# One core, attention and a gated low-rank block: tile 2 projected from split operands, splits reordered, reciprocals kept in a score bank

## The chip, the cores and the metric

The kernel runs on one core of one Trainium2 chip. The metric is the device time of one execution in microseconds (us). The core has TensorE (matrix products, PE in the profile; PEld is its weight load), VectorE (DVE), ScalarE (ACT), GpSimd (POOL) and SyncE (SP), which issues nearly all transfers here. Each engine works through its own list of instructions in order; semaphores tie the lists together.

## The reference, cut to what matters

1,024 tokens (16 batches of 64) of width 512; `c` is the context, 32 query heads of 16 over 8 key/value heads.

```python
h = layernorm(x)
q, k, v = h @ Wq, c @ Wk, c @ Wv          # 512x512, 512x128, 512x128
q, k = rope(q, pos), rope(k, pos)
x = x + softmax(q k^T / 4) v @ Wo
h = layernorm(x)
gate = softmax over the 16 largest of 64 router scores of h
x = x + 2 * (((h @ A.T) * gate) @ B.T)    # 64 experts of rank 8
```

## The kernel before

**Tiles.** The tokens go in T = 8 tiles of 128. Everything is float32. A product is made in one of two ways. *Raw*: one float32 matmul per 128 rows of the contraction, which the profile shows as two records (`raw_q`, `raw_kv`). *Split*: each operand is written as a high part in `float32r` and the rest (`hi`, `lo`), and three matmuls are made per 128 rows: hi x hi, hi x lo, lo x hi (`project_q`, `project_kv`, `project_out`, `project_down`, `up_high`, `up_low`). ScalarE makes the high parts (`split_hi`, `x_high`, `c_high`), GpSimd the low parts of weights and context (`split_lo`, `c_low`), VectorE those of x (`x_low`). `RAW = 3`: tiles 0 to 2 are raw, tiles 3 to 7 split.

**Order.** Each engine's program is written out by hand: `first()`, `second()`, then `step(i)` for i = 1 to 5, then `last()`. `first()` warms TensorE with 12 bf16 matmuls (`keep_warm`), turns tile 0, and projects tiles 0 and 1. `second()` finishes attention of tile 0 and projects tile 2. In `step(i)` attention of tile i is finished, the scores of i+1 are made, tile i+2 is projected, and the last block runs two tiles behind.

**The o chain of a tile.** `values(t)` (TensorE, L1149) writes the weighted values and the sums into score banks 0 and 1; VectorE transposes them into `o_s` (L789), takes reciprocals `inv` (L794), multiplies into `o_t` (L798, two instructions) and transposes into `o_n` (L804); ScalarE makes `oT_hi` (L507), GpSimd `oT_lo` (L313); TensorE then runs `project_out(t)` (L1053, L1054, L1058). `scores(t, b)` writes banks 2 and 3 for b = 0 and banks 0 and 1 for b = 1. Before b = 1 it waits for

```python
pe.wait_ge(o_step, 3 * t - 2)
```

which is the transposition of tile t-1 out of these banks (each tile gives `o_step` three increments: transposition, reciprocals, multiplication).

**The maxima.** `top(t, b)` (VectorE, L771) takes row maxima of the scores, `m_parts` splits them, `turn_m` (L1122) and ScalarE's `m_out` (L492, `mT`) turn them, and `turned_scores(t)` (L1132, L1138) makes the transposed scores less the maxima, of which `exps` (L499) are taken.

**Banks.** `xhT_bank`, `kT_bank` and `values_out` use `RAW` to tell early tiles from later ones. GpSimd's list holds, besides, the standard deviations (`deviation1`, `deviation2`), `rotated_q` (the sum of the two halves of the rotated q, L294), `k_blocks` (L304) and `o_low`. SyncE's list gives the order of all loads but `pos` and `c(0)`, which ScalarE issues.

Of the kernel before, what the change touches and what calls it, by code (L numbers as in the profile page):

```python
# [19 lines left out]
RAW = 3  # L20
# [20 lines left out]
WARM = 12  # L41
# [10 lines left out]
def build(nc, x, cT, pos, wq, wkv, wo, aT, router, bT, out):  # L52
    ctx = ExitStack()
    with ctx:
# [66 lines left out]
        o_s, inv = sb("o_s", [P, 2, HD, 2, HD]), sb("inv", [P, 2, HD])  # L121
# [304 lines left out]
        def _(act):  # L426
# [132 lines left out]
            def first():  # L559
# [39 lines left out]
                m_out(0)
                x_raw(2)  # L600

            def second():
                act.wait_ge(ld_am, 16)
                act.wait_ge(route_ok, 1)
                split_hi(am_hi, am_sb, am_h, 0)
# [3 lines left out]
                for k in range(1, DK):  # L609
                    split_hi(am_hi, am_sb, am_h, k)  # L610
# [87 lines left out]
        def _(dve):  # L698
# [205 lines left out]
            def first():  # L904
                dve.memset(warm[:], 0.0).then_inc(warm_ok, 1)
                dve.wait_ge(ld_pos, 16)
                dve.tensor_copy(pos_f[:], pos_sb[:]).then_inc(rope_step, 1)
                dve.wait_ge(ld_x[0], 16)
                dve.bn_stats(bn1[:], x_sb[:, 0, :]).then_inc(stat1, 1)
# [133 lines left out]
        def _(pe):  # L1043
# [385 lines left out]
```

## Time and profile before

| | |
|---|---|
| median of 3 runs | 175.37 us (175.06 to 175.51) |
| the profiled execution | 174.97 us, of which its span is 173.3 |
| TensorE matmuls busy | 167.6 us (97%), 1440 |
| TensorE weight loads busy | 130.9 us (76%) |
| VectorE busy | 132.6 us (77%), 391 |
| ScalarE busy | 90.3 us (52%), 206 |
| GpSimd busy | 85.2 us (49%), 109 |
| granted TensorE clock | 1.00 in every stretch |

The span is from the first to the last instruction. Busy times overlap, so shares do not add up. Matmuls are pipelined: a row with a start of 26.56 and a length of 1.02 for two records overlaps the next row, and the cost of a group is best read as the distance between its start and that of the next one.

### The profile page before, as it was taken

To read this page: it belongs to the slowest core of one execution; us is meant where nothing else is said; L and a number is where in the kernel's file an instruction comes from. 1 tells how busy PE (TensorE), PEld (TensorE's weight loads), DVE (VectorE), ACT (ScalarE), POOL (GpSimd) and SP (SyncE) were. 2 spreads that over 40 slices of the span, in tenths; PEclk is the share of its full clock that TensorE was granted. 3 is DMA by queue.
4 is the path that set the end of the run, shared out by engine and by line. 5 is a ranking of instruction groups with operands and counts; after the bars stand their busy time and mean duration, and the time that the engine had idled before them with its cause. 6 is when DMAs were issued, how large, how long until landed. Compare 5 with 4: busy or idle time off the path is not lost.

```text
span 173.3 us, 4057 instructions
## 1 busy us (share of the span) xinstructions
PE 167.6 (97%) x1440; PEld 130.9 (76%) x1440; DVE 132.6 (77%) x391; ACT 90.3 (52%) x206; POOL 85.2 (49%) x109
## 2 busy tenths in 40 slices
PE   7999999999989999999999999999999999999994
PEld 2656674577869887888879887888879776889883
DVE  1758857987999899849996699549984998758651
ACT  3478899756468335652837344752528345334210
POOL 5499989599569926423581326402550302422100
PEclk9999999999999999999999999999999999999999
DMA  5999912002102020101001000100001001000013
GB/s 150 319 402 384 407 48 62 0 6 61 62 2 61 4 61 0 62 4 34 29 4 61 0 4 0 64 2 0 4 0 61 4 0 61 4 4 0 0 61 121
DMA packets 5331, 11.30 MB, mean 65 GB/s; under 512 B 688, under 2 KB 944, under 8 KB 5056
## 3 DMA queue, kind: packets, MB, share of 16 engines
q1 hardware_dynamic: 5024, 10.79, 17.9%
q8 instruction: 11, 0.18, 0.4%
q10 hardware_dynamic: 288, 0.27, 0.4%
q14 instruction: 8, 0.07, 0.1%
HBM read 8.95 MB, written 2.10 MB: 64 GB/s over the span
## 4 chain that ended last, share of the span: by engine, by line
PE 86%; DVE 7%; ACT 3%; issue 2%; ACTq 0%; DVEq 0%
PE ps_w L1053 13%; PE ps_w L1054 12%; PE ps_w L1058 12%; PE ps_t L1066 9%; PE ps_s L1113 6%; PE ps_s L1149 5%; PE ps_s L1132 4%; PE ps_w L1206 3%; PE ps_w L1214 3%; PE ps_t L1071 3%; PE ps_w L1046 3%; PE ps_w L1047 3%; PE ps_w L1048 3%; PE ps_s L1054 2%; PE ps_s L1053 2%
## 5 line engine op out<-in xcount | busy, mean ns | idle before, releaser
L313 POOL TENSOR_TENSOR oT_lo<-o_n,oT_hi 128x512 fp32r<-128x512 f32 x8 | 10.3, 1291 | 30.5 <-ACT oT_hi L507 30.5
L771 DVE TENSOR_REDUCE ps_s<-ps_s 128x8 f32<-128x512 f32 x32 | 21.0, 692 | 0.9 <-PE ps_s L1113 0.7
L499 ACT ACTIVATE eT<-ps_s 128x512 f32<-128x512 f32 x32 | 17.0, 600 | 4.1 <-PE ps_s L1138 4.0
L328 POOL TENSOR_TENSOR late<-late,gate 128x512 f32<-128x512 f32 x7 | 7.6, 1081 | 19.7 <-DVE gate L864 19.7
L1053 PE MATMUL ps_w<-am_hi,x2T_hi 128*128 128x288 f32 x48 | 13.9, 312 | 0.0
L1054 PE MATMUL ps_w<-am_lo,x2T_hi 128*128 128x288 f32 x48 | 13.1, 296 | 0.0
L304 POOL TENSOR_TENSOR k_bd_lo<-kT_lo,half_mask 128x512 fp32r<-128x512 f32 x8 | 8.8, 1096 | 7.7 <-DVE kT_lo L743 7.7
L1214 PE MATMUL ps_w<-wq_sb,xT_raw 128*128 128x512 f32 x24 | 11.8, 606 | 0.0
L1053 PE MATMUL ps_w<-wo_hi,oT_hi 128*128 128x512 f32 x28 | 11.3, 405 | 0.4 <-ACT oT_hi L507 0.4
L789 DVE STREAM_TRANSPOSE o_s<-ps_s 128x1024 f32<-128x1024 f32 x8 | 9.9, 1243 | 1.8 <-PE ps_s L1149 1.8
L507 ACT ACTIVATE oT_hi<-o_n 128x512 fp32r<-128x512 f32 x8 | 5.1, 632 | 12.0 <-DVE o_n L804 12.0
L1054 PE MATMUL ps_w<-wo_lo,oT_hi 128*128 128x512 f32 x28 | 11.0, 395 | 0.0
L1053 PE MATMUL ps_w<-b_hi,zT_hi 128*128 128x512 f32 (+1 forms) x28 | 10.8, 392 | 0.0
L492 ACT ACTIVATE mT<-ps_t 128x256 fp32r<-128x256 f32 x8 | 3.1, 384 | 14.7 <-PE ps_t L1122 14.7
L832 DVE TENSOR_TENSOR x2T_lo<-ps_t,x2T_hi 128x512 fp32r<-128x512 f32 x7 | 4.8, 690 | 7.5 <-ACT x2T_hi L520 7.5
L1054 PE MATMUL ps_w<-b_lo,zT_hi 128*128 128x512 f32 (+1 forms) x28 | 10.5, 379 | 0.0
L1113 PE MATMUL ps_s<-k_bd_hi,qT_hi 64*128 64x256 f32 x64 | 10.1, 311 | 0.0
L1053 PEld LDWEIGHTS ps_w<-am_hi,x2T_hi 128*128 128x128 f32 x48 | 9.0, 188 | 1.4 <-issue 0.2
L294 POOL TENSOR_TENSOR q_r<-q_a,q_b 128x512 f32<-128x512 f32 x7 | 9.1, 1293 | 1.4 <-DVE q_b L754 1.4
L1113 PEld LDWEIGHTS ps_s<-k_bd_hi,qT_hi 64*128 64x128 f32 x64 | 6.1, 185 | 4.5 <-issue 4.3
L1113 PE MATMUL ps_s<-k_bd_lo,qT_hi 64*128 64x256 f32 x64 | 9.1, 279 | 0.0
L1054 PEld LDWEIGHTS ps_w<-am_lo,x2T_hi 128*128 128x128 f32 x48 | 9.0, 188 | 0.0
(211 smaller groups left out, 524.9 us busy)
## 6 DMA issues: line engine op xcount, KB each, us to landing
x_sb<-x SPq DMA_DIRECT2D x8, 256.0 KB, 6.9
cT_in<-cT SPq DMA_DIRECT2D x7, 256.0 KB, 3.7
out<-res SPq DMA_DIRECT2D x7, 256.0 KB, 2.0
wq_sb<-wq SPq DMA_DIRECT2D x4, 256.0 KB, 6.2
late<-wo SPq DMA_DIRECT2D x1, 1024.0 KB, 8.2
am_sb<-aT SPq DMA_DIRECT2D x1, 1024.0 KB, 8.4
b_sb<-bT SPq DMA_DIRECT2D x1, 1024.0 KB, 7.0
wkv_sb<-wkv SPq DMA_DIRECT2D x1, 512.0 KB, 4.7
```

Source lines behind the costliest of these rows:

```text
L294: pool.tensor_tensor(q_r[:].rearrange("p (r k d) -> p k r d", r=REP, k=KVH), q_a[:].rearrange("p (k r d) -> p k r d", r=REP, k=KVH), q_b[: ...
L304: pool.tensor_tensor(bd[:, t % 2], kT[:].bitcast(F32).rearrange("p (b q) -> p b q", b=2).unsqueeze(2) .broadcast_to([P, 2, HALF_H, BATCH]) ...
L313: pool.tensor_tensor(oT_lo[:], o_n[:].rearrange("p (b r q) -> p r b q", b=2, r=REP), oT_hi[:].bitcast(F32), ALU.subtract).then_inc(oT_lo_o ...
L499: act.activation(eT[:, c].rearrange("p b n -> p (b n)"), ps_s[:, c, :], ACT.Exp)\
L771: dve.tensor_reduce(neg_top[:, b, HALF_H * half:HALF_H * (half + 1), :], ps_s[:, 2 * (1 - b) + half, :].rearrange("p (r h k) -> p h r k", ...
L789: dve.transpose(o_s[:].rearrange("p h u g d -> p (h u g d)"), ps_o.rearrange("p h n -> p (h n)")).then_inc(o_step, 1)
L1053: pe.matmul(dst, hi(k), w_hi[:, k, cols], start=(k == 0), stop=False)
L1054: pe.matmul(dst, hi(k), w_lo[:, k, cols], start=False, stop=False)
L1058: mm = pe.matmul(dst, lo(k), w_hi[:, k, cols], start=False, stop=(k == DK - 1))
L1066: mm = pe.transpose(dst[:, P * k:P * (k + 1)], src[:, P * k:P * (k + 1)], ident[:])
L1113: mm = pe.matmul(ps_s[:, 2 * (1 - b) + half, 2 * P * rp:2 * P * (rp + 1)], q[rows, t % 2, b, 2 * rp:2 * rp + 2, :].rearrange("p r q -> p ( ...
L1214: return pe.matmul(ps_w0[:], xT_raw[:, k, :], wq_sb[:, k, :], start=(k == 0), stop=(k == DK - 1))
```

## The change

1. `RAW` becomes 2, so tile 2 is projected by `project_kv` and `project_q`; a new `FIRST = 3` takes over where `RAW` told banks and waits apart. `c_high(2)`, `c_low(2)`, `x_high(2)` and `x_low(2)` are new, `x_raw(2)` goes. In `second()` of TensorE two chunks of q lie ahead of `values(0)`, then one, `turn_k(2)`, the last one, both halves of `scores(1)`, `turn_xh(3)` and only then `project_out(0)`.
2. The splits of `wo` and `A` change their order on ScalarE and GpSimd; `value_blocks(1)` comes behind `m_out(0)` and `x_high(2)`; `x_high(3)` ahead of `m_out(1)`.
3. At the start: 11 warm matmuls for 12; half of the raw key/value product of tile 0 before `turn_xh(0)`; all four splits of `wkv` before `x_raw(0)`; the statistics of x ahead of the rope table on VectorE; x(1) is loaded before c(1).
4. The reciprocals of tiles 0 to 5 go into score bank 0 (`inv_of`), and `scores(t, 1)` waits for the multiplication of tile t-1 (`3 * t`) for t up to 6. The rotated q of tile 0 is multiplied in place in its bank.
5. In `step(1)` VectorE runs `x2_low(0)` behind `m_parts(2)`, not ahead of `top(2, 0)`.

```diff
-RAW = 3
+RAW = 2
+FIRST = 3
-WARM = 12
+WARM = 11
...
+        def inv_of(t):
+            return ps_s[:, 0, 0:2 * HD].rearrange("p (h u) -> p h u", h=2) if t < T - 2 else inv_late[:]
...
+            load_x(1)
             load_c(1)
-            load_x(1)
@@ gpsimd first(), second()
-                for k in range(REP - 1):
-                    split_lo(wo_lo, wo_sb, wo_hi, wo_h, wo_l, k)
+                split_lo(wo_lo, wo_sb, wo_hi, wo_h, wo_l, 0)
+                split_lo(wo_lo, wo_sb, wo_hi, wo_h, wo_l, 1)
+                c_low(2)
                 rotated_q(1)
...
+                deviation1(3)
+                split_lo(wo_lo, wo_sb, wo_hi, wo_h, wo_l, 2)
                 split_lo(wo_lo, wo_sb, wo_hi, wo_h, wo_l, 3)
-                deviation1(3)
                 split_lo(am_lo, am_sb, am_hi, am_h, am_l, 0)
+                o_low(0)
                 split_lo(am_lo, am_sb, am_hi, am_h, am_l, 1)
-                o_low(0)
@@ scalar first(), second()
-                split_hi(wkv_hi, wkv_sb, wkv_h, 0)
-                split_hi(wkv_hi, wkv_sb, wkv_h, 1)
+                for k in range(DK):
+                    split_hi(wkv_hi, wkv_sb, wkv_h, k)
                 x_raw(0)
-                split_hi(wkv_hi, wkv_sb, wkv_h, 2)
-                split_hi(wkv_hi, wkv_sb, wkv_h, 3)
...
                 normalise(2)
+                c_high(2)
                 split_hi(wo_hi, wo_sb, wo_h, 2)
                 split_hi(wo_hi, wo_sb, wo_h, 3)
+                m_out(0)
+                x_high(2)
                 value_blocks(1)
-                m_out(0)
-                x_raw(2)
...
-                split_hi(am_hi, am_sb, am_h, 0)
                 for c in range(PAIRS):
                     exps(0, c)
                 q_high(1)
-                for k in range(1, DK):
+                for k in range(DK):
                     split_hi(am_hi, am_sb, am_h, k)
...
+                x_high(3)
                 m_out(1)
-                x_high(3)
@@ vector first(), step()
-                rotate_q(0)
+                dve.wait_ge(q_ps, 1)
...
+                dve.tensor_tensor(w, w, table(0, 0, H), ALU.mult).then_inc(q_rot, 1)
                 dve.wait_ge(q_rot, 2)
                 dve.tensor_tensor(q_r[:].rearrange("p (r k d) -> p k r d", r=REP, k=KVH),
-                                  q_a[:].rearrange("p (k r d) -> p k r d", r=REP, k=KVH),
+                                  ps_w0[:].rearrange("p (k r d) -> p k r d", r=REP, k=KVH),
...
                 rotate_q(1)
+                x_low(2)
                 statistics1(3)
...
                 rotate_k(p)
-                if f < 0:
-                    x2_low(g)
                 top(n, 0)
...
                     m_parts(n)
+                    x2_low(g)
                     rotate_q(p)
@@ tensor scores(), first(), second()
-                        pe.wait_ge(o_step, 3 * t - 2)
+                        pe.wait_ge(o_step, 3 * t if t < T - 1 else 3 * t - 2)
...
+                pe.wait_ge(ld_wkv, 16)
+                raw_kv(0, [0, 1])
                 turn_xh(0)
-                pe.wait_ge(ld_wkv, 16)
-                raw_kv(0)
+                raw_kv(0, [2, 3]).then_inc(kv_ps, 1)
...
                 turned_scores(0)
-                raw_kv(2)
-                pe.wait_ge(x_raw_ok, 3)
+                project_kv(2)
+                pe.wait_ge(x_lo_ok, 1)
                 turn_q(1)
-                raw_q(2, 0)
+                pe.wait_ge(q_rot, 4)
+                project_q(2, [0, 1])
                 values(0)
-                raw_q(2, 1)
+                project_q(2, [2])
                 turn_k(2)
-                raw_q(2, 2)
+                project_q(2, [3]).then_inc(q_ps, 1)
                 scores(1, 0)
-                raw_q(2, 3).then_inc(q_ps, 1)
                 scores(1, 1)
                 pe.wait_ge(v_st_ok, 3)
+                pe.wait_ge(qT_lo_ok, 2)
+                turn_xh(3)
                 project_out(0)
                 pe.wait_ge(kT_lo_ok, 3)
                 turn_m(1)
-                pe.wait_ge(qT_lo_ok, 2)
-                turn_xh(3)
```

## Rows read from the trace of the kernel before

**Rows 1.** The page: the chain that ended last, by engine.

```profile
PE 86%; DVE 7%; ACT 3%; issue 2%; ACTq 0%; DVEq 0%
```

**Rows 2.** Windows: length, busy us (instructions) of the engines, granted clock, DMA.

```profile
39.00:52.90 13.90, 13.23 (x140) 10.35 (x140) 12.71 (x33) 8.06 (x19) 10.13 (x12) 1.00 0.14 39
71.23:90.63 19.40, 19.40 (x183) 16.25 (x183) 15.82 (x48) 10.05 (x23) 8.21 (x10) 1.00 0.09 30
```

**Rows 3.** Timeline of TensorE, `second()`: start, length, instruction, [idle before].

```profile
24.29 1.99 PE L1206 MATMUL ps_w<-wkv_sb,cT_in 128*128 128x256 f32 x8
...
26.12 0.60 PE L1066 MATMUL ps_t<-ident,q_r 128*128 128x128 f32 x4
...
26.56 1.02 PE L1214 MATMUL ps_w<-wq_sb,xT_raw 128*128 128x512 f32 x2
...
27.52 1.09 PE L1149 MATMUL ps_s<-eT,v_bd 64*32 64x256 f32 x32
...
33.87 0.47 PE L1053 MATMUL ps_w<-wo_hi,oT_hi 128*128 128x512 f32 x1 [0.37 <-ACT oT_hi L507]
```

**Rows 4.** Timeline of TensorE, split products of tile 3 and what follows each.

```profile
39.06 0.47 PE L1046 MATMUL ps_w<-wq_hi,xT_hi 128*128 128x512 f32 x1 [0.26 <-DVE xT_lo L718]
...
41.33 1.09 PE L1149 MATMUL ps_s<-eT,v_bd 64*32 64x256 f32 x32
...
43.20 0.37 PE L1053 MATMUL ps_w<-wkv_hi,cT_hi 128*128 128x256 f32 x1
...
44.80 0.39 PE L1113 MATMUL ps_s<-k_bd_hi,qT_hi 64*128 64x256 f32 x2
```

**Rows 5.** Timeline, GpSimd's splits and VectorE's multiplications of tile 0.

```profile
28.90 2.79 POOL L271 TENSOR_TENSOR am_lo<-am_sb,am_hi 128x576 fp32r<-128x576 f32 x2
...
30.40 1.91 DVE L798 TENSOR_TENSOR o_t<-o_s,inv 128x256 f32<-128x256 f32 x2
```

**Rows 6.** Tiles o_t and q_r: duration ns min/median/max, first and last start.

```profile
L798 DVE TENSOR_TENSOR o_t<-o_s,inv x16: 411/422/1574, 30.4 to 147.7; 128x256 f32<-128x256 f32 x16
...
L950 DVE TENSOR_TENSOR q_r<-q_a,q_b x1: 1018/1018/1018, 13.9 to 13.9; 128x512 f32<-128x512 f32 x1
```

**Rows 7.** Timeline of the start, and the landing of c(0) after its issue.

```profile
1.21 0.46 ACTq L428 DMA_DIRECT2D cT_in<-cT  x1
...
DMA to landing us min/median/max: 4.9/4.9/4.9
...
1.24 5.30 PE L1071 MATMUL ps_t<-warm 128*128 128x512 bf16 x12 [1.24 <-DVE warm L905]
...
7.07 1.89 PE L1206 MATMUL ps_w<-wkv_sb,cT_in 128*128 128x256 f32 x8
...
15.53 1.10 PE L1235 MATMUL ps_s<-eT 16*128 16x64 f32 x8
```

**Rows 8.** Timeline of ScalarE in `second()`, and GpSimd's last block of keys.

```profile
27.26 1.82 ACT L431 ACTIVATE am_hi<-am_sb 128x576 fp32r<-128x576 f32 x3
...
33.09 0.63 ACT L507 ACTIVATE oT_hi<-o_n 128x512 fp32r<-128x512 f32 x1 [1.19 <-DVE o_n L804]
...
41.33 1.03 POOL L304 TENSOR_TENSOR k_bd_lo<-kT_lo,half_mask 128x512 fp32r<-128x512 f32 x1
```

**Rows 9.** Timeline of TensorE, `step(1)` into `step(2)`: `turn_m(2)` and `project_down(0)`.

```profile
50.87 0.41 PE L1122 MATMUL ps_t<-ident,m_split 128*128 128x128 f32 x2 [0.57 <-DVE m_split L783]
...
52.89 0.40 PE L1053 MATMUL ps_w<-am_hi,x2T_hi 128*128 128x288 f32 x1
```

**Rows 10.** Timeline, multiplication and first scores of b = 1, `step(1)` and `step(3)`.

```profile
44.67 0.76 DVE L798 TENSOR_TENSOR o_t<-o_s,inv 128x256 f32<-128x256 f32 x2
...
45.61 0.28 PE L1113 MATMUL ps_s<-k_bd_hi,qT_hi 64*128 64x256 f32 x2
...
81.01 0.76 DVE L798 TENSOR_TENSOR o_t<-o_s,inv 128x256 f32<-128x256 f32 x2
...
82.09 0.28 PE L1113 MATMUL ps_s<-k_bd_hi,qT_hi 64*128 64x256 f32 x2
```

More of the change, by code:

```diff
@@ L120, in build @@
         router_sb = eT[0:ROUTER].rearrange("p c b n -> p (c b n)")[:, 0:D + E]
-        o_s, inv = sb("o_s", [P, 2, HD, 2, HD]), sb("inv", [P, 2, HD])
+        o_s, inv_late = sb("o_s", [P, 2, HD, 2, HD]), sb("inv_late", [P, 2, HD])
         o_t, o_n = sb("o_t", [P, HD, 2, HD]), sb("o_n", [P, D])
@@ L169, in xhT_bank @@
         def xhT_bank(t):
-            return ps_t1 if t == 1 or t > RAW else ps_t0
+            return ps_t1 if t == 1 or t > FIRST else ps_t0
         def kT_bank(t):
-            return (ps_t1 if t < RAW else ps_t0)[:, 0:P]
+            return (ps_t1 if t < FIRST else ps_t0)[:, 0:P]
         def mT_bank(t):
@@ L453, in values_out @@
                 act.wait_ge(kv_ps, t + 1)
-                if t < RAW:
+                if t < FIRST:
                     act.wait_ge(k_rot, 3 * t + 3)
@@ L726, in rotate_k @@
                 dve.wait_ge(kv_ps, t + 1)
-                if t >= RAW:
+                if t >= FIRST:
                     dve.wait_ge(v_st_ok, t + 1)
@@ L793, in attend @@
                 for h in range(2):
-                    mm = dve.reciprocal(inv[:, h, :], o_s[:, h, :, 1 - h, 0])
+                    mm = dve.reciprocal(inv_of(t)[:, h, :], o_s[:, h, :, 1 - h, 0])
                 mm.then_inc(o_step, 1)
@@ L798, in attend @@
                     mm = dve.tensor_tensor(o_t[:, :, h, :], o_s[:, h, :, h, :],
-                                           inv[:, h, :].unsqueeze(2).broadcast_to([P, HD, HD]), ALU.mult)
+                                           inv_of(t)[:, h, :].unsqueeze(2).broadcast_to([P, HD, HD]), ALU.mult)
                 mm.then_inc(o_step, 1)
@@ L905, in first @@
                 dve.memset(warm[:], 0.0).then_inc(warm_ok, 1)
+                dve.wait_ge(ld_x[0], 16)
+                dve.bn_stats(bn1[:], x_sb[:, 0, :]).then_inc(stat1, 1)
                 dve.wait_ge(ld_pos, 16)
                 dve.tensor_copy(pos_f[:], pos_sb[:]).then_inc(rope_step, 1)
-                dve.wait_ge(ld_x[0], 16)
-                dve.bn_stats(bn1[:], x_sb[:, 0, :]).then_inc(stat1, 1)
+                dve.wait_ge(stat1, 1)
+                dve.bn_aggr(mv1[:], bn1[:]).then_inc(stat1, 1)
+                dve.wait_ge(stat1, 2)
+                dve.tensor_scalar_add(ve1[:], mv1[:, 1:2], EPS).then_inc(stat1, 1)
                 dve.wait_ge(rope_step, 1)
@@ L913, in first @@
                                   freq[:].unsqueeze(1).broadcast_to([P, T, J]), ALU.mult).then_inc(rope_step, 1)
-                dve.wait_ge(stat1, 1)
-                dve.bn_aggr(mv1[:], bn1[:]).then_inc(stat1, 1)
                 dve.wait_ge(rope_step, 2)
@@ L918, in first @@
                    .then_inc(rope_step, 1)
-                dve.wait_ge(stat1, 2)
-                dve.tensor_scalar_add(ve1[:], mv1[:, 1:2], EPS).then_inc(stat1, 1)
                 dve.wait_ge(rope_step, 3)
@@ L978, in step @@
                 f, g, n, p = i - 2, i - 1, i + 1, i + 2
-                if p > RAW:
+                if p > FIRST:
                     x_low(p)
@@ L1199, in up_low, with raw_kv @@
                 low_part(up_of(t), chunk(zT_of(t)[1]), b_hi, slice(0, D)).then_inc(up_ps, 1)
-            def raw_kv(t):
+            def raw_kv(t, chunks=range(DK)):
                 pe.wait_ge(ld_c[t], 16)
@@ L1204, in raw_kv @@
                     pe.wait_ge(v_st_ok, t)
-                for k in range(DK):
+                for k in chunks:
                     mm = pe.matmul(ps_w1[:, 0:2 * KV], cT_in[:, t % 2, k, :], wkv_sb[:, k, :],
                                    start=(k == 0), stop=(k == DK - 1))
-                mm.then_inc(kv_ps, 1)
+                return mm
             def raw_q(t, k):
                 pe.wait_ge(x_raw_ok, t + 1)
-                if t >= 1:
+                if t == 1:
+                    pe.wait_ge(q_r_ok, 1)
+                elif t >= 2:
                     pe.wait_ge(q_rot, 2 * t)
@@ L1228, in first @@
                 mm.then_inc(q_ps, 1)
-                raw_kv(1)
+                raw_kv(1).then_inc(kv_ps, 1)
                 pe.wait_ge(kT_lo_ok, 1)
```

5 lines of the change are left out of this document (added).

## The prediction

> **What bounds the kernel now.** I read the chain that ended last first [rows 1]: 86% of the span is TensorE. The reader should see that this is no wait but work. The windows [rows 2] then say where it is not so: in a full step (71.23 to 90.63) TensorE has no gap at all, while in the first step behind the prologue (39.00 to 52.90) it has 0.67 us of gaps and VectorE is busy for 12.71 of 13.90 us. So a gain must come as TensorE work taken away, or as gaps before 53 us, and whatever has been won at the first `project_down` (52.89, [rows 9]) is carried to the end, because the steps after it are full. I follow that one instant through the change.
>
> **Tile 2 from split operands.** A raw chunk of q is two records, 26.56 to 27.52, 0.96 us with the change of tiling behind it [rows 3]. Three split chunks (nine matmuls) run 39.06 to 41.33 [rows 4], 0.76 each: 0.2 less, four times 0.8. Raw keys and values take 24.29 to 26.12, 1.83; split ones 43.20 to 44.80, 1.60: 0.23 less. TensorE work falls by 1.0 us in `second()`. New on the others: `c_high(2)` and `c_low(2)` (0.63 on ScalarE; as 512-wide subtraction about 1.3 on GpSimd) and `x_low(2)` (0.69 on VectorE). GpSimd gives `c_low` the place of a `wo` split, VectorE stands idle before `rotate_k(2)` for longer than that, and ScalarE's copy lies ahead of `m_out(0)`, from where `value_blocks(1)` (1.09) goes. I cost these three at nothing; without that cover `c_low` would hold the product up by its 1.3.
>
> **Where the o chain starts.** `values(0)` stood behind one raw q chunk; now two split ones are ahead. From `turned_scores(0)` on: 0.23 less for keys and values, 1.50 - 0.96 = 0.54 more for q, so 0.3 later. The start (below) brings 0.3 earlier. `values(0)` stays at about 27.5.
>
> **Reciprocals in a score bank.** In tile 0 the two multiplications by `inv` take 1.91 us; the usual one is 0.42, the longest 1.57 [rows 5, 6]. GpSimd runs two `am_lo` splits through that time, and its row is not lengthened (2.79 for two). What a multiplication with one operand in PSUM costs beside GpSimd is not shown directly. Bounds: 0 saved (it stays blocked) and 1.91 - 0.84 = 1.07 saved. Other VectorE rows with one PSUM operand under GpSimd work are undisturbed (`xT_lo` 0.69), which is why I take 1.07. The Trainium skill (SBUF — State Buffer, "SBUF: two separate sides") says that a VectorE instruction with two SBUF inputs and a GpSimd one exclude each other for a whole instruction; by that rule one operand in PSUM frees the multiplication and the full 1.07 is saved; by the long row alone, whose cause it does not name, it is anything from 0 to 1.07. `o_n` would then be there at 31.9 to 32.0 instead of 33.05.
>
> **What is late next.** ScalarE. It had been idle for 1.19 us before `oT_hi` [rows 8], so its queue ended at 31.90. One more `am_hi` split (1.82 / 3 = 0.61) now lies ahead of `o_high(0)`; `q_high(1)` starts some 0.1 earlier. So `oT_hi` starts at 31.9 + 0.6 - 0.1 = 32.4 to 32.5, not 33.09: 0.65 gained of 1.07. TensorE has less work and waits there longer (`project_out(0)` at 33.2 for 33.87 [rows 3]); `turn_xh(3)` (0.45) fills some of it. `k_low(2)` waits for ScalarE's `kT_hi` at the same place, so VectorE gains only 0.5: maxima, `m_parts(1)`, then `rotate_q(2)` end at 37.1. GpSimd: `wo_lo` 2 and 3 are through at 30.0, before they are wanted at 33.2.
>
> **The wait for `xT_lo`.** TensorE waited until 39.06 for it [rows 4]. `turn_xh(3)` now runs before `project_out(0)` and `x_high(3)` before `m_out(1)`, so `x_low(3)` follows `rotate_q(2)` directly: 37.1 to 37.8. `turned_scores(1)` starts with `mT`, 0.65 earlier, and ends at 38.0. The product starts at 38.05: 1.0 gained. `values(1)` then also needs four exponentials, 2.07 behind the turned scores: 40.4 instead of 41.33 [rows 4], 0.9 gained. GpSimd is 0.9 later (three `am_lo` splits behind `o_low(0)`): `k_bd` of tile 2, ready at 42.36 [rows 8], ends at 43.25, and the scores want it at 44.80 - 0.9 = 43.9. Hidden by 0.65; beyond that it costs its excess.
>
> **Step 1.** `x2_low(0)` moves from before the maxima to behind `m_parts(2)`. That takes away the wait at `turn_m(2)`, whose transposes started at 50.87, 0.57 behind a gap [rows 9]; but `turn_xh(4)` now waits for `x2_low(0)`, and `project_down(0)` waits for the residual, behind the same VectorE work as before, unbroken from 42.53. So this edit moves no more than the 0.4 us TensorE lay behind VectorE. With VectorE 0.9 earlier: the residual at 52.5 - 0.9 = 51.6, `turned_scores(2)` done at 51.5, `project_down` at 51.75 to 51.85 for 52.89. Gained: 1.05 to 1.15.
>
> **The start.** One warm matmul less is 0.43. But `cT_in` lands at 1.21 + 4.9 = 6.11 [rows 7], so the first half of the keys and values starts at 6.2, 0.15 before the transposes did (6.36). The windows give a granted clock of 1.00 from the first instruction on, and yet the twelve warm matmuls of 512 columns stand 0.43 apart (5.30 for twelve, 0.63 of it the last one's own), which is the 1.2 GHz level. The raw keys and values at 7.07 go at the fast one (eight records, 1.73 from start to start of what follows). So the rate doubled in the 0.7 us of transposes between, after five and a half us of matmuls. In the changed kernel the first records of the half product lie there: about 0.3 lost, and q starts at 8.7 instead of 8.80. The Trainium skill (TensorE: Matmul & The Clock Gate, "Part 1: The HAM clock gate") has the number of slow matmuls at a kernel's start differ from run to run; the trace has one run and cannot show it. Then `q_r` of tile 0: with one operand in PSUM about 0.69 for 1.02 [rows 6], one multiplication of the three dependent now: ready 0.3 earlier. Router at 15.2 for 15.53 [rows 7]: 0.3. The order of the statistics gives 0.1 inside that. The order of x and c on the queue brings x(1) earlier, but `xh(1)` waits behind GpSimd's `wq_lo` splits: nothing; c(1) comes later by one transfer, still ahead of the raw product at 12.35.
>
> **Full steps.** `scores(t, 1)` now waits for the multiplication of the tile before. In a full step that ends at 81.77 and the scores start at 82.09 [rows 10]; in step 1, 45.43 and 45.61. I cost it at nothing, by 0.32 and 0.18 us of cover, five tiles.
>
> **Sum.** 0.3 at the start; 0.3 given back at `values(0)`; 0.65 at `oT_hi`; 0.35 more at `xT_lo`; 0.1 lost to the exponentials; 0.15 in step 1: 1.05 us. The profiled execution took 174.97 (span 173.3 and 1.67 around it), so 173.9, span 172.25; the median of the runs shown is 0.40 higher: **174.3**.
>
> **Rivals.**
> *The o chain does not get free, or ScalarE eats it* (gain 0 to 0.5, centre 175.1). If the multiplication stays at 1.57, or ScalarE's longer queue (a later `value_blocks(1)`, a wait for `q_r`) ends at 33, only the start and part of the `xT_lo` wait remain: 0.3. For it: ScalarE is the limit by my own account. Against: its queue is counted from rows of equal work.
> *More* (1.5 to 2.2, centre 173.6): if the slow rate ends earlier at the start (0.3), and the 0.67 of gaps [rows 2] goes whole. Against: VectorE's unbroken work.
> *Slower: `scores(t, 1)` waits in each step.* It costs 0 up to 0.32 us of lateness, and all beyond it, five times. Were the multiplication 1.57 in every step: 5 x (1.15 - 0.32) = 4.2, less 1.05: 178.5. It decides from 0.32 + 1.05 / 5 = 0.53 us of lateness. Against: in full steps GpSimd is idle then, and the reciprocals write 16 elements only.
>
> **Chances.** Forecast 0.52 (its own range 173.8 to 174.8), absorbed 0.22, more 0.13, slower or about even for reasons of waits 0.13. 0.3% (0.53 us) is about what a measurement can tell. Faster: 0.52 + 0.13, and a little of the second: 0.67; the same: 0.23; slower: 0.10. The range takes in "more" down to 1.9 us and the absorbed case whole: 173.5 to 175.4.
>
> **What the profile would show.** Right: both `o_t` multiplications near 0.42 in tile 0; `oT_hi` of tile 0 near 32.4, with ScalarE busy until then; the first split q product of tile 3 at 38.05; `project_down` of tile 0 at 51.8; full steps 19.4 long. Wrong: `oT_hi` after 33; a gap before the second half of the scores; q of tile 0 starting after 8.8; `k_bd` of tile 2 holding up the scores.

## The result, and the profile after

The changed kernel takes 173.41 us (median of 5 runs, 173.26 to 173.83) beside 175.17 us (5 runs, 175.06 to 175.51) for the kernel before on the same chip: ratio 0.9904, 95% interval 0.9887 to 0.9921, so 1.76 us or 1.0% faster. The direction was forecast; the size was not: 1.05 us was worked out, and 173.41 lies 0.09 below the range. Of the 0.89 us between the forecast of 174.3 and 173.41, 0.2 is the starting point: the forecast was counted from 175.37, the median of three runs, and all five give 175.17. The other 0.7 is a gain that the sum did not hold. The two profiled executions alone differ by 1.14 us (173.83 and 174.97), because the profiled one of the changed kernel was the slowest of its five, while the one shown of the kernel before lies below all five of its timed runs.

From the page of the changed kernel: its span, the shares of the chain that ended last (the row that answers to [rows 1]) and the busy times.

```profile
span 172.1 us, 4074 instructions
...
PE 166.9 (97%) x1447; PEld 131.5 (76%) x1447; DVE 132.1 (77%) x392; ACT 90.4 (53%) x207; POOL 86.2 (50%) x110
...
PE 88%; DVE 4%; DMA 3%; issue 2%; ACT 1%; ACTq 0%; DVEq 0%
```

TensorE still sets the end; its matmul time fell by 0.7 us. Its windows, with the columns of [rows 2]: the first step behind the prologue, a full step, and the first 5 us.

```profile
38.22:51.77 13.55, 13.45 (x143) 10.40 (x139) 12.09 (x32) 8.07 (x18) 11.31 (x13) 1.00 0.12 40
70.10:89.51 19.41, 19.41 (x182) 16.26 (x180) 15.82 (x48) 10.06 (x24) 8.22 (x10) 1.00 0.11 30
0.00:5.00 5.00, 3.76 (x9) 1.35 (x10) 1.49 (x6) 1.49 (x2) 2.50 (x24) 1.00 0.54 202
```

The gaps of the first step are down from 0.67 to 0.10 us; the full step is 19.41 us long and full, as before. The timeline of TensorE, the rows that answer to [rows 3, 4, 7, 9] (start, duration, what runs, the wait before it in brackets):

```profile
1.24 4.88 PE L1081 MATMUL ps_t<-warm 128*128 128x512 bf16 x11 [1.24 <-DVE warm L909]
6.39 1.44 PE L1216 MATMUL ps_w<-wkv_sb,cT_in 128*128 128x256 f32 x4 [0.28 <-DMA cT_in<-cT]
7.67 0.60 PE L1076 MATMUL ps_t<-ident,xh 128*128 128x128 f32 x4
9.04 2.81 PE L1226 MATMUL ps_w<-wq_sb,xT_raw 128*128 128x512 f32 x6
15.66 1.10 PE L1248 MATMUL ps_s<-eT 16*128 16x64 f32 x8
27.83 1.09 PE L1159 MATMUL ps_s<-eT,v_bd 64*32 64x256 f32 x32
33.19 0.47 PE L1063 MATMUL ps_w<-wo_hi,oT_hi 128*128 128x512 f32 x1
38.22 0.50 PE L1056 MATMUL ps_w<-wq_hi,xT_hi 128*128 128x512 f32 x1
43.98 0.39 PE L1123 MATMUL ps_s<-k_bd_hi,qT_hi 64*128 64x256 f32 x2
51.77 0.41 PE L1063 MATMUL ps_w<-am_hi,x2T_hi 128*128 128x288 f32 x1
```

And of the other engines, with all rows of ScalarE ahead of `oT_hi` (they answer to [rows 5, 8]):

```profile
29.62 0.80 ACT L449 ACTIVATE xh<-x_sb,shift,rstd 128x512 f32<-128x512 f32 x1
30.31 1.42 POOL L275 TENSOR_TENSOR am_lo<-am_sb,am_hi 128x576 fp32r<-128x576 f32 x1
30.33 0.25 ACT L464 ACTIVATE v_st<-ps_w 128x128 f32<-128x128 f32 x1
30.61 1.09 ACT L474 ACTIVATE v_bd<-v_st 64x64 f32<-64x64 f32 x4
30.72 0.75 DVE L802 TENSOR_TENSOR o_t<-o_s,ps_s 128x256 f32<-128x256 f32 x2
31.73 0.63 ACT L444 ACTIVATE cT_hi<-cT_in 128x512 fp32r<-128x512 f32 x1
32.27 0.26 ACT L484 ACTIVATE kT_hi<-ps_t 128x128 fp32r<-128x128 f32 x1
32.42 0.62 ACT L513 ACTIVATE oT_hi<-o_n 128x512 fp32r<-128x512 f32 x1
37.15 0.68 DVE L722 TENSOR_TENSOR xT_lo<-ps_t,xT_hi 128x512 fp32r<-128x512 f32 x1
42.03 1.05 POOL L308 TENSOR_TENSOR k_bd_lo<-kT_lo,half_mask 128x512 fp32r<-128x512 f32 x1
```

From `oT_hi` (32.42 for a forecast of 32.4 to 32.5) to `project_down` (51.77 for 51.75 to 51.85) all stands where it was forecast, or within 0.2 us of it (the split product of tile 3 at 38.22 for 38.05, held by `turned_scores(1)`, which had waited for `mT`). The start does not: the half product starts at 6.39, not 6.2, q at 9.04, not 8.7, and the router product at 15.66, not 15.2. It is 0.13 later than in [rows 7], not 0.3 earlier. So a path that began 0.46 late ended on time. Right readings of two instants hid a wrong one of what lies between them.

### The profile page after: what moved, and what is told of

It is laid out like the page before. It is cut to its first block, busy times and chain, and to the rows that moved or that the text cites. A ratio compares the mean times of both kernels' runs of the same rounds, so it can differ in the third digit from the quotient of the medians.

```text
span 172.1 us, 4074 instructions
## 1 busy us (share of the span) xinstructions
PE 166.9 (97%) x1447; PEld 131.5 (76%) x1447; DVE 132.1 (77%) x392; ACT 90.4 (53%) x207; POOL 86.2 (50%) x110
## 4 chain that ended last, share of the span: by engine, by line
PE 88%; DVE 4%; DMA 3%; issue 2%; ACT 1%; ACTq 0%; DVEq 0%
PE ps_w L1063 13%; PE ps_w L1064 12%; PE ps_w L1068 12%; PE ps_t L1076 9%; PE ps_s L1123 7%; PE ps_s L1159 5%; PE ps_s L1142 4%; PE ps_w L1226 4%; PE ps_w L1056 3%; PE ps_w L1057 3%; PE ps_w L1058 3%; DMA cT_in<-cT 3%; PE ps_w L1216 2%; PE ps_s L1064 2%; PE ps_s L1063 2%
## 5 line engine op out<-in xcount | busy, mean ns | idle before, releaser
L308 POOL TENSOR_TENSOR k_bd_lo<-kT_lo,half_mask 128x512 fp32r<-128x512 f32 x8 | 8.3, 1043 | 7.2 <-DVE kT_lo L747 7.2
L1056 PE MATMUL ps_w<-wq_hi,xT_hi 128*128 128x512 f32 x24 | 10.4, 433 | 0.0
L1057 PE MATMUL ps_w<-wq_lo,xT_hi 128*128 128x512 f32 x24 | 9.5, 395 | 0.0
L1058 PE MATMUL ps_w<-wq_hi,xT_lo 128*128 128x512 f32 x24 | 9.5, 394 | 0.0
```

Source lines behind the costliest of these rows:

```text
L1056: pe.matmul(dst, hi(k), w_hi[:, k, cols], start=(k == 0), stop=False)
L1057: pe.matmul(dst, hi(k), w_lo[:, k, cols], start=False, stop=False)
L1058: mm = pe.matmul(dst, lo(k), w_hi[:, k, cols], start=False, stop=(k == DK - 1))
```

## What the runs showed

Thirteen variants ran, and each of the two kernels once more (e4, e8), 5 to 12 times each, in four sessions with 11 to 22 runs of the kernel before in each. Differences between variants of two sessions, e4 among them, carry up to 0.06 us from the session besides the spread. The most useful reading is a subtraction. Three instants of each profiled execution are the start of the router product (R), the start of `oT_hi` of tile 0 (O), and the first `project_down` (D); the end of the span is E.

| kernel | R | O - R | D - R | E - R | median us |
|---|---|---|---|---|---|
| before | 15.53 | 17.56 | 37.36 | 157.8 | 175.37 |
| e1_start_only | 15.07 | 17.57 | 37.38 | 157.7 | 174.75 |
| e9_loads_only | 15.58 | 17.56 | 37.37 | 157.7 | 175.05 |
| changed | 15.66 | 16.76 | 36.11 | 156.4 | 173.41 |
| e4_after_again | 15.43 | 16.85 | 36.18 | 156.5 | 173.45 |
| e2_no_start | 16.24 | 16.83 | 36.16 | 156.5 | 174.21 |
| e11_whole_product | 15.53 | 16.85 | 36.18 | 156.6 | 173.49 |
| e12_x1_early | 14.80 | 16.78 | 36.12 | 156.5 | 173.41 |
| e3_inv_sbuf | 15.33 | 17.47 | 36.68 | 157.1 | 174.03 |
| e5_x2_back | 15.23 | 16.78 | 36.44 | 156.6 | 173.58 |
| e6_all_but_tile2 | 15.08 | 16.41 | 36.64 | 157.2 | 174.29 |

R moves from one execution to the next; for one and the same kernel behind it, what follows does not, to 0.1 us. (The second profile of the kernel before, e8, is left out: its clock fell behind R, see the last section.) That splits the gain in two: 1.3 us behind the router product (157.75 less 156.45), and the rest ahead of it.

### The start, alone and taken away

e1_start_only is the kernel before with all of the start; e2_no_start is the changed kernel with the old start.

```diff
--- e1_start_only against the kernel before (e2 reverses all of it in the changed one)
-WARM = 12
+WARM = 11
...
-            load_c(1)
             load_x(1)
+            load_c(1)
@@ scalar: the four wkv splits ahead of x_raw(0)
@@ vector: bn_stats, bn_aggr, ve of x(0) ahead of the rope table
...
-                rotate_q(0)
+                dve.tensor_tensor(w, w, table(0, 0, H), ALU.mult).then_inc(q_rot, 1)
@@ tensor
-                turn_xh(0)
-                raw_kv(0)
+                raw_kv(0, [0, 1])
+                turn_xh(0)
+                raw_kv(0, [2, 3]).then_inc(kv_ps, 1)
@@ tensor raw_q(1): it now waits until q_r of tile 0 is made, since q of tile 0 stays in its bank
```

> The kernel before with the start alone (11 warm matmuls, half product ahead of the transposes, all wkv splits first, statistics first, x(1) before c(1), q of tile 0 in place). Two theories of why the median fell by 1.76 us and the profiled execution by 1.14. S: the instant at which TensorE's rate doubles differs from one execution to the next; the profiled one of the changed kernel had it late (first four raw records 1.44 us for 0.86), so the start is worth 0.3 to 0.6 us in the median: 174.6 to 174.9. M: the start is worth nothing and the middle more than I counted: 175.1 to 175.3.

> The changed kernel with the start as before (12 warm matmuls, transposes ahead of the whole product, old orders, q of tile 0 through q_a). S: 173.7 to 174.1, the middle's 1.1 to 1.4 us. M: 173.4 to 173.5. In its profile turned_scores of tile 0 starts at 23.15 as before and project_down of tile 0 at 51.6 to 52.0.

> The changed kernel once more, for a second profile. S: if the first four raw records take less than the 1.44 us of the first profile, everything behind them is earlier by as much: router before 15.66, project_down of tile 0 before 51.77, span under 172.1, each by the same amount to 0.1. M: the start may move, but project_down of tile 0 stays at 51.8, since VectorE sets it. Median 173.4.

> The kernel before once more, for a second profile. Median 175.2. S: its first transposes and the start of the raw product may stand at another time than 6.36 and 7.07, and the rest of the program follows by 0 to 0.3 us, less than in the changed kernel, because only transposes lie in the slow stretch and xh(1) waits for GpSimd.

Measured (before: 175.35): e1 174.75 (11 runs, 174.53 to 174.99), ratio 0.9962 [0.9948, 0.9976], 0.60 us. e2 174.21 (6 runs, 173.87 to 174.56), 0.9926 [0.9903, 0.9950]. e4, the changed kernel again, 173.45 (6 runs, 173.29 to 173.94), 0.9893 [0.9871, 0.9915], so the start is worth 0.76 us inside the changed kernel. e8, the kernel before again, 175.30 (12 runs, 175.05 to 177.13), 1.0002 [0.9980, 1.0024]. Priced at 0.3, the start gives 0.6 to 0.76. Theory M is out: e1 is clear of the kernel before. What S names is there: in e4 the first four raw records take 1.10 us from start to start for 1.28, q starts at 8.58 for 9.04, and R comes 0.23, `project_down` 0.16 and the span 0.2 earlier. But half of those 0.46 us are gone again at R, and the profile of e2 has `project_down` at 52.40, not at 51.6 to 52.0, although q of tile 0 starts at 8.54 there, as early as in e4. The instant of doubling is not the main part of the start.

Where it goes is seen at tile 1. The rows of e2: the statistics of x(1), the instruction of GpSimd that needs them, and the transposes of TensorE.

```profile
11.95 0.69 DVE L712 BATCH_NORM_STATS2 bn<-x_sb 128x6 f32<-128x512 f32 x1 [2.12 <-DMA x_sb<-x]
13.13 0.56 POOL L282 TENSOR_TENSOR rstd<-ve,neg_half 128x1 f32<-128x1 f32 x1 [0.68 <-DVE ve L720]
15.04 0.63 PE L1072 MATMUL ps_t<-ident,xh 128*128 128x128 f32 x4 [1.07 <-ACT xh L449]
```

The same of e8:

```profile
11.83 0.69 DVE L706 BATCH_NORM_STATS2 bn<-x_sb 128x6 f32<-128x512 f32 x1 [1.94 <-DMA x_sb<-x]
13.01 0.56 POOL L278 TENSOR_TENSOR rstd<-ve,neg_half 128x1 f32<-128x1 f32 x1 [0.50 <-DVE ve L714]
```

GpSimd waits for the data here, and TensorE for `xh(1)`: 1.07 us in e2, 0.89 in e8. In the profile that the prediction rests on, of the kernel before, nothing waited for x(1):

```profile
11.15 0.69 DVE L706 BATCH_NORM_STATS2 bn<-x_sb 128x6 f32<-128x512 f32 x1 [1.06 <-DMA x_sb<-x]
12.42 0.56 POOL L278 TENSOR_TENSOR rstd<-ve,neg_half 128x1 f32<-128x1 f32 x1
```

GpSimd was at `wq_lo` until 12.4, and the statistics need 1.18 us (e2: 11.95 to 13.13), so they were ready at 12.33. This is what "nothing" was read from: a margin of 0.1 us. Over all profiles the old order of the loads has x(1) at 11.15, 11.56, 11.83 and 11.95 (before, e10, e8, e2), and GpSimd waiting 0, 0.37, 0.50 and 0.68 us; the new one has it at 10.65 to 11.44, median 10.80 (eleven profiles), and GpSimd waiting at most 0.22. e4 has x(1) at 11.35, late for the new order, and TensorE's wait is 0.32:

```profile
14.44 0.63 PE L1076 MATMUL ps_t<-ident,xh 128*128 128x128 f32 x4 [0.32 <-ACT xh L449]
```

### The reciprocals and x2_low

```diff
--- e3_inv_sbuf against the changed kernel
-            return ps_s[:, 0, 0:2 * HD].rearrange(...) if t < T - 2 else inv_late[:]
+            return inv_late[:]
...
-                        pe.wait_ge(o_step, 3 * t if t < T - 1 else 3 * t - 2)
+                        pe.wait_ge(o_step, 3 * t - 2)
--- e5_x2_back against the changed kernel
+                if f < 0:
+                    x2_low(g)
                 top(n, 0)
...
-                    x2_low(g)
```

> The changed kernel with the reciprocals in SBUF for all tiles and the old wait of scores(t, 1). If the operand in PSUM is what freed the multiplication: one of the two of tile 0 takes about 1.4 us again, because an am_lo split runs from 30.3 to 31.7, oT_hi starts near 33.3 for 32.42, and 0.6 to 0.85 us are lost: 174.0 to 174.3. Rival, the new order of the splits alone freed it: 0.42 each, and 173.4.

> The changed kernel with x2_low(0) ahead of the maxima of tile 2 again. By my count the move gives 0.15 us at project_down of tile 0 (VectorE's work up to the residual is the same): 173.5 to 173.7. Rival: the move is worth its whole 0.6 us of earlier maxima: 174.0.

Measured (before: 175.41): e3 174.03 (6 runs, 173.85 to 174.36), 0.9923 [0.9895, 0.9951]: 0.58 us lost against e4, 0.5 of it behind the router product (D - R 36.68 for 36.11 to 36.18). The rows of e3, timeline and then the tile `o_t`:

```profile
29.98 1.43 POOL L275 TENSOR_TENSOR am_lo<-am_sb,am_hi 128x576 fp32r<-128x576 f32 x1
30.40 1.62 DVE L802 TENSOR_TENSOR o_t<-o_s,inv_late 128x256 f32<-128x256 f32 x2
32.80 0.63 ACT L513 ACTIVATE oT_hi<-o_n 128x512 fp32r<-128x512 f32 x1 [0.53 <-DVE o_n L808]
...
L802 DVE TENSOR_TENSOR o_t<-o_s,inv_late x16: 411/422/1285, 30.4 to 147.1; 128x256 f32<-128x256 f32 x16
```

And the tile `o_t` of the changed kernel, for [rows 6]:

```profile
L802 DVE TENSOR_TENSOR o_t<-o_s,ps_s x12: 414/418/423, 30.7 to 119.3; 128x256 f32<-128x256 f32 x12
```

With both operands in SBUF one multiplication of 0.42 us takes 1.29 while GpSimd makes an `am_lo` split. With the reciprocals in PSUM the longest of twelve takes 0.423, the first two of them beside the same split (30.31 to 31.73 in the changed kernel). The rival, that the new order of the splits freed it, falls with e3, and again with e6 below, where the order is the old one. The Trainium skill (SBUF — State Buffer, "SBUF: two separate sides") has such an exclusion for a whole instruction, with two SBUF inputs on VectorE; these rows agree.

e5 173.58 (6 runs, 173.43 to 173.84), 0.9898 [0.9873, 0.9924]: 0.13 us against e4, inside the spread of either. The trace says more: D - R is 0.26 to 0.33 longer than in the changed kernel, but E - R only 0.1. The full steps behind it give part of it back.

### All but tile 2

e6_all_but_tile2 is e1 with the reciprocals in the bank and `x2_low` moved; tile 2 stays raw, and `second()` keeps its old order.

```diff
--- e6_all_but_tile2 against e1_start_only
-                    mm = dve.reciprocal(inv[:, h, :], o_s[:, h, :, 1 - h, 0])
+                    mm = dve.reciprocal(inv_of(t)[:, h, :], o_s[:, h, :, 1 - h, 0])
...
+                        pe.wait_ge(o_step, 3 * t if t < T - 1 else 3 * t - 2)
...
+                    x2_low(g)
```

> The kernel before with the start, the reciprocals in the score bank and the move of x2_low(0), but tile 2 raw and second() and the splits in their old order. oT_hi of tile 0 is early by 1.07, but TensorE's raw work ends at 33.4, so project_out(0) gains 0.45 only and xT_lo comes behind it. 174.2 to 174.6. If the raw work is not what holds it: 173.6.

Measured 174.29 (7 runs, 174.05 to 174.74; before: 175.41), 0.9938 [0.9915, 0.9961]: 0.46 us better than e1, 0.84 worse than e4. Its timeline:

```profile
28.46 2.80 POOL L274 TENSOR_TENSOR am_lo<-am_sb,am_hi 128x576 fp32r<-128x576 f32 x2
29.96 0.75 DVE L799 TENSOR_TENSOR o_t<-o_s,ps_s 128x256 f32<-128x256 f32 x2
31.49 0.63 ACT L510 ACTIVATE oT_hi<-o_n 128x512 fp32r<-128x512 f32 x1
32.98 0.49 PE L1059 MATMUL ps_w<-wo_hi,oT_hi 128*128 128x512 f32 x1
...
37.36 0.69 DVE L719 TENSOR_TENSOR xT_lo<-ps_t,xT_hi 128x512 fp32r<-128x512 f32 x1 [1.13 <-ACT xT_hi L452]
38.20 0.47 PE L1052 MATMUL ps_w<-wq_hi,xT_hi 128*128 128x512 f32 x1 [0.26 <-DVE xT_lo L719]
...
51.72 0.40 PE L1059 MATMUL ps_w<-am_hi,x2T_hi 128*128 128x288 f32 x1
```

Here `oT_hi` comes 1.15 us earlier after the router product than before, the full amount that the multiplications lost (1.91 - 0.75 = 1.16), since no fourth `am_hi` split lies ahead. But TensorE is at the raw product and the scores of tile 1 until 32.98, so `project_out(0)` starts only 0.44 us earlier after the router product than before (17.90 for 18.34), and `x_low(3)` is late: it waits 1.13 us for `xT_hi`, because `turn_xh(3)` and `x_high(3)` keep their old places here. No run tells this order from the split form of tile 2.

The two halves of the change behind the router product do most of their work alone. The reciprocals with `x2_low` give 0.46 us without tile 2 (e1 to e6); tile 2 with its orders and `x2_low` gives 0.72 without the reciprocals (e1 to e3); both together give 1.30 (e1 to e4). With `x2_low`, 0.13, counted once, that leaves 0.1 to 0.25 us that only the pair gives, about the spread of the runs.

### The order at the start, piece by piece

```diff
--- e7_c0_first against the changed kernel
-            act.dma_start(pos_sb[:], pos).then_inc(ld_pos, 16)
             act.dma_start(cT_in[:, 0], cT[0]).then_inc(ld_c[0], 16)
+            act.dma_start(pos_sb[:], pos).then_inc(ld_pos, 16)
--- e9_loads_only against the kernel before (e10_old_loads reverses it in the changed one)
-            load_c(1)
             load_x(1)
+            load_c(1)
--- e11_whole_product against the changed kernel
-WARM = 11
+WARM = 12
@@ scalar: the wkv splits in their old order around x_raw(0)
-                raw_kv(0, [0, 1])
                 turn_xh(0)
-                raw_kv(0, [2, 3]).then_inc(kv_ps, 1)
+                raw_kv(0).then_inc(kv_ps, 1)
--- e12_x1_early against the changed kernel
             for k in range(DK):
+                if k == 3:
+                    load_x(1)
...
-                split_lo(wq_lo, wq_sb, wq_hi, wq_h, wq_l, 1)
                 deviation1(1)
+                split_lo(wq_lo, wq_sb, wq_hi, wq_h, wq_l, 1)
--- e13_q_copy against the changed kernel
-                dve.tensor_tensor(w, w, table(0, 0, H), ALU.mult).then_inc(q_rot, 1)
+                rotate_q(0)
@@ tensor raw_q(1): it waits for the rotation of q of tile 0 again, not for q_r
--- e14_old_stats against the changed kernel
-                dve.bn_stats(bn1[:], x_sb[:, 0, :]).then_inc(stat1, 1)
                 dve.tensor_copy(pos_f[:], pos_sb[:]).then_inc(rope_step, 1)
+                dve.bn_stats(bn1[:], x_sb[:, 0, :]).then_inc(stat1, 1)
... (bn_aggr and ve go back between the steps of the rope table)
--- e15_x1_early_whole: e12 with the edit of e11
```

> The changed kernel with c(0) issued ahead of the positions on ScalarE's queue. c(0) lands 0.4 earlier, before the warm matmuls end at 6.11; the half product starts at 6.15 for 6.39. S: a part of that is at the slow rate; 0.1 to 0.25 us gained, 173.2. Rival: VectorE's rope table, now behind a later landing of the positions, takes it back: 173.4 or more.

> The kernel before with x(1) issued ahead of c(1), nothing else. My working had this at nothing, from one profile in which x(1) landed at 11.1. Two later profiles of the old order have it at 11.8 and 11.9, and GpSimd waits 0.50 and 0.68 us for the statistics. Theory L, the order of the loads is the larger part of the start: 174.8 to 175.0 (0.3 to 0.6 gained). Theory P, it is TensorE's half product and the shorter warm-up: 175.3.

> The changed kernel with c(1) ahead of x(1) again. L: 173.8 to 174.0, GpSimd waiting for the statistics of tile 1 in the profile. P: 173.5.

> The changed kernel with 12 warm matmuls, the transposes of tile 0 ahead of the whole key/value product and the old order of the wkv splits on ScalarE; the loads, VectorE's order and q in place stay changed. L: 173.4 to 173.6, since TensorE waits for xh(1) afterwards anyway. P: 173.8 or more.

> The changed kernel with x(1) issued ahead of the last chunk of wq and the deviation of tile 1 ahead of the second wq_lo split on GpSimd. x(1) lands near 10.3, xh(1) is ready near 13.2 for 14.4, the turn of tile 1 follows the second raw product without a wait, and q of tile 0 (14.5) is late next: 0.1 to 0.35 us gained, 173.1 to 173.3. Rival: the last chunk of wq lands later than TensorE wants it (11.4) and the gain is gone: 173.4 or more.

> The changed kernel with q of tile 0 through q_a and a sum of two SBUF tiles again. If this is what remains of the start: the sum takes 1.02 us for 0.69 beside GpSimd's k_bd, turn_q(0) follows 0.2 to 0.35 us later, median 173.6 to 173.8. Rival: turn_xh(1) is late anyway and hides it, 173.4 to 173.5.

> The changed kernel with VectorE's old order at the start (positions first, statistics between the steps of the rope table). The table is then 0.0 to 0.1 earlier and xh(0) 0.1 later, and neither is waited for: 173.4 to 173.5. Rival: x(0) lands first and GpSimd's splits hang on the table's end: 173.6 or more.

> x(1) ahead of the last chunk of wq and the early deviation, with 12 warm matmuls and the transposes ahead of the whole product. If the spread of the x1-early kernel (172.99 to 173.80) comes from raw records in the slow stretch, this one is narrower, 172.9 to 173.4, with a median of 173.1 to 173.2. Rival: the spread comes from the landings, and the median stays at 173.4.

Measured (before: 175.41), to be read against e4's 173.45:

| | runs | median | ratio | against 173.45 |
|---|---|---|---|---|
| e7_c0_first | 12 | 174.85 (174.72 to 176.63) | 0.9975 [0.9942, 1.0008] | +1.40 |
| e9_loads_only, beside 175.41 | 12 | 175.05 (174.91 to 176.55) | 0.9992 [0.9971, 1.0013] | |
| e10_old_loads | 5 | 173.84 (173.77 to 173.92) | 0.9914 [0.9899, 0.9928] | +0.39 |
| e11_whole_product | 5 | 173.49 (173.33 to 173.89) | 0.9901 [0.9886, 0.9917] | +0.04 |
| e12_x1_early | 5 | 173.41 (172.99 to 173.80) | 0.9894 [0.9876, 0.9912] | -0.04 |
| e13_q_copy | 6 | 173.58 (173.36 to 173.84) | 0.9884 [0.9853, 0.9915] | +0.13 |
| e14_old_stats | 6 | 173.45 (173.38 to 173.56) | 0.9878 [0.9848, 0.9909] | 0 |
| e15_x1_early_whole | 6 | 173.29 (172.96 to 173.68) | 0.9871 [0.9836, 0.9906] | -0.16 |

Only the loads show by themselves: 0.39 us in the changed kernel. The intervals of e10 and e4 overlap, and e4 is of another session (counted from each session's kernel before it is 0.33), but all five runs of e10 lie at 173.77 or above, where only 2 of 11 runs of the changed kernel do, and its trace has the wait that theory L names (GpSimd 0.37 us, TensorE 0.50). In the kernel before the medians of the two orders differ by 0.36 (e9), but the ratio's interval takes in 1, so that one is not settled; its profile, with x(1) at 11.29, is no earlier than the one of the kernel before. The half product with 11 warm matmuls is worth nothing (e11), and neither is VectorE's order (e14). The product in place saves 0.4 us of VectorE time (e13's sum of the halves takes 1.13 us at 13.62 for 0.69) and at most 0.13 of the kernel's. The 0.7 of the whole start is then 0.4 for the loads and some 0.1 for q; the last 0.2 lies inside the spread of the runs and stays open.

e7 missed its forecast of 173.2 by 1.65 us, the largest miss of all. It was meant to bring c(0) earlier, and did: it lands at 4.4 for 5.7 (e4), and the half product starts right behind the warm matmuls, at 5.91. But the position numbers then land last, at 5.7 for 3.8. Its timeline:

```profile
5.79 0.17 DVE L913 CAST pos_f<-pos_sb 128x8 f32<-128x8 int32 x1 [0.90 <-DMA pos_sb<-pos]
7.62 0.66 PE L1076 MATMUL ps_t<-ident,xh 128*128 128x128 f32 x4 [0.57 <-DVE xh L930]
8.53 2.84 POOL L275 TENSOR_TENSOR wkv_lo<-wkv_sb,wkv_hi 128x256 fp32r<-128x256 f32 x4 [1.64 <-DVE abs_r L941]
...
13.78 0.57 POOL L282 TENSOR_TENSOR rstd<-ve,neg_half 128x1 f32<-128x1 f32 x1
15.71 0.63 PE L1076 MATMUL ps_t<-ident,xh 128*128 128x128 f32 x4 [1.14 <-ACT xh L449]
```

VectorE works its list in order, so `xh` of tile 0 waits behind a cast that it does not need. That costs TensorE 0.57 us, and yet q starts at 9.06, as in the first profile of the changed kernel (9.04), so the loss lies behind it. The rope table ends late too (`abs_r` at 8.22 for 6.72 in e4), and GpSimd's list waits for it before the `wkv_lo` splits: they start at 8.53 for 7.02, the deviation of tile 1 behind them at 13.78 for 12.53, without any wait for x(1), and TensorE waits 1.14 us for `xh(1)`. R is 16.70 for 15.43. So 1.4 us are lost to a transfer of 4 KB. The rival had named the rope table, but at "173.4 or more", and not the way it takes, through GpSimd.

e12 asks whether more can be had by sending x(1) ahead of the last chunk of `wq`:

```profile
10.09 0.69 DVE L711 BATCH_NORM_STATS2 bn<-x_sb 128x6 f32<-128x512 f32 x1 [0.44 <-DMA x_sb<-x]
13.54 0.60 PE L1077 MATMUL ps_t<-ident,xh 128*128 128x128 f32 x4
```

In this execution R is 14.80 and the time 172.99, but the median is 173.41, outside the 173.1 to 173.3 that were expected: GpSimd and TensorE no longer wait for x(1), and what is left varies with the rest of the start. e15, e12 with e11's start, has 173.29, no narrower than e12 (0.72 us from lowest to highest for 0.81), so neither of its two readings is shown, and its runs overlap those of the changed kernel. No version here is shown to beat it. What makes this spread stays open.

## Why the prediction was right in direction and short in size

**Right.** The chain of work from ScalarE's `oT_hi` to `project_down`: O to D took 19.80 us before, and takes 19.33 to 19.35; the forecast was 19.25 to 19.45 (51.75 to 51.85 less 32.4 to 32.5). The multiplications fell from 1.91 to 0.75, a little more than the bound of 1.07 had it, `xT_lo` runs from 37.15, and the scores of tile 2 find `k_bd_lo` ready (it ends at 43.08, they start at 43.98). What was won at `project_down` is carried: from there to the end all kernels take 120.1 to 120.6 us. The full step is 19.41 us, so the rival "slower" (the wait in `scores(t, 1)`) fell, and with it "absorbed". "More" names 1.5 to 2.2 us, which is what came. Of its two reasons one held in part (the gaps of the first step fell from 0.67 to 0.10 us), the other is not borne out in the profiled execution (the rate doubled at about 7.0 us, no earlier than before), and the rest comes from neither but from the two steps below. That the profiled `oT_hi` and `project_down` stood at their forecast instants was luck: the start was 0.46 us later than forecast and the path behind it 0.4 to 0.5 shorter.

**First step that failed: "ScalarE ... `oT_hi` starts at 31.9 + 0.6 - 0.1".** The row of 31.90 is of an execution with the router product at 15.53. The prediction moved the router product to 15.2, but left ScalarE's queue where it was, as if it did not begin with the same start. e1 shows that it does. The end of the queue in the kernel before, and then the rows of e1:

```profile
31.65 0.26 ACT L478 ACTIVATE kT_hi<-ps_t 128x128 fp32r<-128x128 f32 x1
...
31.18 0.26 ACT L478 ACTIVATE kT_hi<-ps_t 128x128 fp32r<-128x128 f32 x1
32.64 0.63 ACT L507 ACTIVATE oT_hi<-o_n 128x512 fp32r<-128x512 f32 x1 [1.19 <-DVE o_n L802]
```

The queue ends at 31.44, 16.37 us behind its router product at 15.07; before it was 31.91 - 15.53 = 16.38. Counted from there, `oT_hi` should have come at 16.38 + 0.6 - 0.1 = 16.9 us behind the router product; measured are 16.76 to 16.85, with ScalarE busy up to it, as forecast. With 15.2 for the router that is 32.1, not 32.4 to 32.5. The terms "0.3 given back at `values(0)`" and "0.65 at `oT_hi`" together gained 0.35 us; measured is 17.56 less 16.76 to 16.85, 0.7 to 0.8. So 0.4 us is missing from the sum here: the start's 0.3 was given back at a place that no longer set the time.

**Second: "The order of x and c on the queue brings x(1) earlier, but `xh(1)` waits behind GpSimd's `wq_lo` splits: nothing".** Measured 0.39 us (e10). The sentence is true of the one execution it was read from, where x(1) came at 11.15 with a margin of 0.1 us. In e10, e8 and e2 the same transfer in the same place of the queue came at 11.56, 11.83 and 11.95, and GpSimd waited 0.37, 0.50 and 0.68 us for it. The term of the start, 0.3, measured 0.60 alone (e1) and 0.76 inside the changed kernel (e2 against e4).

**The sum by the runs.** 1.3 us behind the router product (forecast 37.36 - (51.8 - 15.2) = 0.76) and 0.6 ahead of it (forecast 0.3): 1.9, for which e4 measured 1.90 and the first comparison 1.76. By parts: the start 0.60 (e1), the reciprocals and `x2_low` 0.46 more (e6), tile 2 and the orders that go with it 0.84 more (e4). Taken away one by one, the reciprocals are worth 0.58 (e3) and `x2_low` 0.13 (e5); the sum of these two is larger than 0.46, as it would be if TensorE, without the changes of tile 2, cannot use all of the earlier `oT_hi`; the difference of 0.25 is about the spread of the runs.

**And the comparison of profiles.** The profiled execution of the changed kernel has a late start (15.66; e4 has 15.43), that of the kernel before an early one (15.53; e8 has 16.11). That is why two profiled executions showed 1.14 us, near the forecast, where the medians show 1.76: a match that confirmed nothing.

## What to carry to other kernels

Count every queue from the same origin: if the sum moves the start by 0.3 us, each engine whose list begins there moves too, and an absolute time from the old trace may only be used after it has been moved. Where a transfer lands closer to the moment at which it would be waited for than its landings differ between executions (here a margin of 0.1 us against 0.8), one execution says nothing about its price; look at a second execution, or put the difference into the range. And compare traces from an instant behind the noisy part: here the distance from the router product repeats to 0.1 us, where whole times differ by 0.5.

## What the runs showed of the hardware that had not been expected

- TensorE's rate at the start. The granted clock is recorded as 1.00 in the first 5 us (last window above), and yet the warm matmuls of 512 columns go 0.43 us apart, which is the 1.2 GHz level. The instant of doubling is not fixed: in the changed kernel it lies at about 7.0 (of the first four raw records, 1.28 us from start to start where a half of [rows 7]'s eight took 0.87, the first lasts 0.77 us, and the last two the usual 0.38, from 7.23 on), while e8's twelve warm matmuls take 4.06 in all, so it fell among them, at about 4. The Trainium skill (TensorE: Matmul & The Clock Gate, "Part 1: The HAM clock gate") has the number of slow matmuls at a start differ from run to run; the runs agree.
- The same 256 KB transfer at the same place of the queue landed 6.7, 7.2, 7.6 and 7.7 us after its issue in four executions (before, e10, e8, e2).
- In e8's profiled execution, with a span of 175.4 us, the granted clock fell by itself. Its windows:

```profile
17.00:19.00 2.00, 2.00 (x6) 0.59 (x7) 1.47 (x4) 1.81 (x6) 2.00 (x3) 0.64 1.10 418
18.00:20.00 2.00, 2.00 (x11) 1.22 (x12) 0.47 (x3) 1.60 (x4) 1.90 (x4) 0.50 1.07 430
19.00:22.00 3.00, 3.00 (x27) 2.62 (x28) 1.50 (x3) 0.90 (x4) 2.90 (x4) 0.67 0.98 389
```

The first and the last window mix two levels: between 18 and 20 us the granted clock is 0.50, the 1.2 GHz level, and TensorE's first scores there start 0.21 us apart for the usual 0.12. The distance from R to the end is 1.5 us longer than in the other profile of this kernel. Of 14 to 17 us TensorE had been busy for 2.11 there, and for 2.90 in the other profile; the DMA engines were as full in that one (shares of 1.11 and 0.98 in the same two windows, clock 1.00), so they alone do not make the difference. No other profiled execution of these kernels has it, and the cause stays open. Five unprofiled runs have a mean clock of 0.988 to 0.994 and take 176.55 to 177.35 us; they are of the kernel before, e7 and e9, none of the changed kernel. e8's other rows are used only up to 16 us.
